# Expert routing in a fused graph network: one list of rows per expert, with the tile tables made in four portions

## The reference

```
x = x + L0_gnn(layernorm(x))     # relational graph convolution, 8 relations
x = x + L0_ffn(layernorm(x))     # feed-forward on the better-scored half of the nodes
x = x + L1_gnn(layernorm(x))     # graph attention, 4 heads
x = x + L1_ffn(layernorm(x))     # 8 experts, each node goes to its best 2

def _L1_ffn_ref(x, Wg, bg, W1, b1, W2, b2):
    gate_scores = x @ Wg + bg
    _, idx = jax.lax.top_k(gate_scores, 2)
    mask = jax.nn.one_hot(idx, 8).sum(axis=-2)
    h = jax.nn.gelu(einsum('td,edh->teh', xf, W1) + b1, approximate=False)   # 256 -> 512
    y = einsum('teh,ehd->ted', h, W2) + b2                                   # 512 -> 256
    return einsum('ted,te->td', y, mask)
```

## Time and profile before

| what | value |
|---|---|
| median of three executions | 6457.74 us |
| the profiled execution's own time | 6457.05 us |
| its span, first to last instruction | 6455.3 us |
| last stage (experts) in the span | from about 5370 us on |
| slots 0 to 19, 20 to 52, tiles after the slots | up to about 5513, to about 5850, to the end |

### The profile page before, as it was taken

How to read it: one execution, slowest core, us unless ns; L and a number is a source line. 1 busy time by engine, 2 the same in 40 slices (tenths; PEclk the granted TensorE clock), 3 DMA queues, 4 the chain that set the end, 5 groups by cost and what they waited for, 6 DMA issues and landing times. The chain is left out here.

```text
span 6455.3 us, 114956 instructions
## 1 busy us (share of the span) xinstructions
PE 4682.2 (73%) x25385; PEld 4006.7 (62%) x25386; DVE 3914.5 (61%) x11536; ACT 1836.6 (28%) x4850; POOL 4211.0 (65%) x4619
## 2 busy tenths in 40 slices
PE   9965555555555557599647777777777766899999
PEld 4435555555555556489635665665666656888998
DVE  5565555555555556733377777777777777663332
ACT  3310000000000003333234444444444444673333
POOL 1247777777777776334577777777777764785444
PEclk9987777777777778799867777767677775999999
DMA  8853333333333335411254444444444435664444
GB/s 310 318 199 104 105 105 105 104 105 105 104 104 105 105 104 166 134 42 49 85 145 117 117 117 117 117 117 117 117 117 117 117 102 171 155 156 91 72 71 67
DMA packets 366348, 786.59 MB, mean 122 GB/s; under 512 B 88338, under 2 KB 224482, under 8 KB 352612
## 3 DMA queue, kind: packets, MB, share of 16 engines
q0 software_dynamic: 209088, 520.50, 30.9%
q1 hardware_dynamic: 129524, 147.11, 7.7%
q10 hardware_dynamic: 27440, 116.02, 4.8%
HBM read 565.20 MB, written 222.43 MB: 122 GB/s over the span
## 5 line engine op out<-in xcount | busy, mean ns | idle before, releaser
L373 POOL DMA_INDIRECT s_rows<-rel_table,s_staged x1664 | 1579.8, 949 | 525.2 <-issue 485.6
L1289 POOL DMA_INDIRECT s_rows<-xp_table,s_index x1664 | 1591.4, 956 | 507.0 <-issue 444.6
L399 PE MATMUL s_part<-s_pick,s_rows 128*128 128x128 f32 x6656 | 1196.7, 353 | 909.3 <-DMA s_rows<-rel_table,s_staged 713.3
L399 PEld LDWEIGHTS s_part<-s_pick,s_rows 128*128 128x128 f32 x6656 | 1108.6, 260 | 997.9 <-DVE s_pick L407 948.8
L1412 PE MATMUL s_part<-s_pick,s_scaled 128*128 128x128 f32 x6656 | 1416.0, 369 | 373.9 <-DVE s_scaled L1577 352.9
L1412 PEld LDWEIGHTS s_part<-s_pick,s_scaled 128*128 128x128 f32 x6656 | 1182.0, 260 | 573.9 <-issue 273.2
L420 DVE TENSOR_TENSOR sums<-sums,s_part 128x256 f32 x1666 | 702.6, 422 | 930.6 <-PE s_part L399 751.5
L1592 DVE SCALAR_TENSOR_TENSOR sums<-sums,s_old_share,s_part 128x256 f32 x1666 | 794.4, 477 | 357.9 <-PE s_part L1412 221.0
L1325 ACT ACTIVATE s_apart<-window,s_local 128x128 f32<-128x128 f32 x1664 | 531.6, 390 | 1151.1 <-PE s_part L1412 1093.5
L1577 DVE TENSOR_TENSOR s_scaled<-s_rows,s_psW 128x256 f32<-128x256 f32 x1664 | 679.6, 408 | 80.7 <-issue 79.8
L407 DVE TENSOR_SCALAR s_pick<-window,s_local,s_weight 128x128 f32<-128x128 f32 x1669 | 625.5, 375 | 13.9 <-issue 0.2
(11 more groups left out here) (346 smaller groups left out, 5392.1 us busy)
## 6 DMA issues: line engine op xcount, KB each, us to landing
rel_table<-s_rows ACTq DMA_DIRECT2D x98, 1024.0 KB, 4.2
sums<-exp_rows SPq DMA_DIRECT2D x224, 132.0 KB, 2.1
s_rows<-rel_table,s_staged POOLq DMA_INDIRECT x1664, 2.7
s_rows<-xp_table,s_index POOLq DMA_INDIRECT x1664
s_edges<-edge_rows SPq DMA_DIRECT2D x208, 80.0 KB
xp_table<-s_xp ACTq DMA_DIRECT2D x49, 264.0 KB, 2.6
x_rows<-s_skip SPq DMA_DIRECT2D x49, 259.0 KB, 3.4
s_x<-in_x SPq DMA_DIRECT2D x98, 128.0 KB
```

Of the source, the lines that this page charges most:

```text
L373: pool.indirect_dma_start(out=rows[:, s, :], out_offset=None, in_=rel_table[:, :], in_offset=bass.IndirectOffsetOnAxis(ap=staged[:, 2 * s ...
L399: mm = pe.matmul(part[s % PARTS][:, k, :], rows[:, s, k * P:(k + 1) * P], pick[:, s % PICKS, :], start=True, stop=True)
L1289: pool.indirect_dma_start(out=rows[:, b * BATCH + s, :], out_offset=None, in_=xp_table[0:NR, :], in_offset=bass.IndirectOffsetOnAxis(ap=in ...
```

## The change

There is now one list per expert over all pairs, and the blank rows come once, at the very end. The table of tiles is written in four portions, when 7, 16, 25 and all 49 pairs are counted. A portion before the last holds only tiles that are already whole in the lists; how many tiles of each expert earlier portions took is kept in `taken`. The tile counts are fixed: up to 21, 57, 93 and 212 tiles. Tiles run in slots from `OPEN = 11` on, 84 of them inside the slots, 128 after.

Since two neighbouring tiles of the first 93 can hold the same node with no blank tile between, each of the first 94 adds waits until the add before it has landed. GpSimd's order in a slot becomes: add, root, two scatters, add, two scatters; the scatters are those of pair q - 3 and `moved` has five buffers. The expert weights are loaded one expert per slot in slots 0 to 7. Three of the four result buffers move to the other half of `sums`. The tables' tile numbers come from an existing constant (`window`). The last portion's eight blank writes stay where they were in SP's last slot. In the first stage, one set of blank rows is written in place of two.

```diff
-A_PAIRS = 15
-GROUP_END = [A_PAIRS, PAIRS]
-GROUP_TILES = [4 * A_PAIRS + 2 * X - 2, 4 * (PAIRS - A_PAIRS) + 2 * X - 2]
-TILES = sum(GROUP_TILES)
-LATE = 4
-SLOTS9 = PAIRS + LATE
-OPEN = A_PAIRS + LATE + 1
+CAP = NR + 2 * P
+GROUP_END = [7, 16, 25, PAIRS]
+PORTIONS = len(GROUP_END)
+TILES = 2 * NT + 2 * X
+TILES_TO = [4 * n - X + 1 for n in GROUP_END[:-1]] + [TILES]
+TILES_FROM = [0] + TILES_TO[:-1]
+SLOTS9 = PAIRS + 4
+OPEN = GROUP_END[0] + 4
-MOVED = 6
+MOVED = 5
...
# SP, slot q
-                        if q == OPEN - 2:
-                            group_in(0)
-                            for k in range(RING - 1):
-                                load_tile(k, 0, k)
-                        if q % 2 == 0 and 1 <= q // 2 <= X:
-                            load_expert(q // 2 - 1)
+                        if q < X:
+                            load_expert(q)
...
-                        if q == A_PAIRS + 2:
-                            blanks(0)
+                        if q == GROUP_END[0] + 2:
+                            group_in(0)
+                            for k in range(RING):
+                                load_tile(k, k)
+                        for g in range(1, PORTIONS - 1):
+                            if q == GROUP_END[g] + 3:
+                                group_in(g)
                         if q == SLOTS9 - 1:
-                            blanks(1)
+                            blanks()
...
# POOL
                         pool.wait_ge(ids_kept, t + 1)
-                        wait_past(pool, y_out[b], 16 * i)
+                        if isinstance(t, int) and t <= TILES_FROM[-1]:
+                            wait_past(pool, y_out[1 - b], 16 * ((t + 1) // 2))
+                        else:
+                            pool.wait_ge(y_out[b], 16 * i)
...
-                        if t is not None and t > 0:
-                            add_tile(t - 1)
-                        if 0 <= q - LATE < PAIRS:
-                            scatter(q - LATE)
                         if t is not None:
                             add_tile(t)
                         if q + 1 < PAIRS:
                             root(q + 1)
+                        if 0 <= q - 3 < PAIRS:
+                            scatter(q - 3, 0)
+                        if t is not None:
+                            add_tile(t + 1)
+                        if 0 <= q - 3 < PAIRS:
+                            scatter(q - 3, 1)
...
# VectorE, the tables of portion g
                     def tiles_of_group(g):
+                        shift = P.bit_length() - 1
+                        v.wait_ge(group_counted, g + 1)
+                        then(v.tensor_scalar(many_i[:, :], count[:, g, :], 0.0 if g + 1 < PORTIONS else float(P - 1), None, ALU.add))
+                        then(v.tensor_scalar(many_i[:, :], many_i[:, :], shift, None, ALU.logical_shift_right))
                         then(v.tensor_copy(many[:, :], many_i[:, :]))
+                        then(v.tensor_tensor(leap[:, :], many[:, :], taken[:, g, 1:X + 1], ALU.subtract))
+                        then(v.tensor_tensor(many[:, :], many[:, :], taken[:, g, 0:X], ALU.subtract))
+                        if g + 1 == PORTIONS:
+                            then(v.tensor_scalar(many[:, :], many[:, :], 1.0, None, ALU.add))
+                            then(v.tensor_scalar(leap[:, :], leap[:, :], 1.0, None, ALU.add))
                         then(v.tensor_tensor_scan(end[:, :], ones[0:1, 0:X], many[:, :], 0.0, ALU.mult, ALU.add))
+                        if g + 1 < PORTIONS:
+                            n = TILES_TO[g] - TILES_FROM[g]
+                            then(v.tensor_tensor(room[:, :], many[:, :], end[:, :], ALU.subtract))
+                            then(v.tensor_scalar(room[:, :], room[:, :], float(n), 0.0, ALU.add, ALU.max))
+                            then(v.tensor_tensor(room[:, :], room[:, :], many[:, :], ALU.min))
+                            then(v.tensor_tensor(taken[:, g + 1, 0:X], taken[:, g, 0:X], room[:, :], ALU.add))
...
-                        if q == GROUP_END[0] + 2:
-                            tiles_of_group(0)
-                            experts_of_tiles(0)
-                        if q == GROUP_END[0] + 3:
-                            rows_of_tiles(0)
+                        for g in range(PORTIONS):
+                            if q == GROUP_END[g] + 2:
+                                tiles_of_group(g)
+                                if g == 0:
+                                    v.wait_ge(unturned, OPEN + 1)
+                                experts_of_tiles(g)
+                                if g in (0, PORTIONS - 1):
+                                    rows_of_tiles(g)
+                            if q == GROUP_END[g] + 3 and 0 < g < PORTIONS - 1:
+                                rows_of_tiles(g)
```

More of the change, by code:

```diff
@@ L100, in gnn_kernel @@
     xp_table = dram("xp_table", [NR + P, EXT])
-    exp_rows = [dram(f"exp_rows{g}", [X * GROUP_CAP[g] + X * P, EXT]) for g in range(2)]
-    blank_rows = [dram(f"blank_rows{g}", [3 * P, EXT]) for g in range(2)]
+    exp_rows = dram("exp_rows", [X * CAP + X * P, EXT])
+    blank_rows = dram("blank_rows", [3 * P, EXT])
     edge_rows = dram("edge_rows", [CHUNKS, 5, P])
@@ L220, in _ @@
                     sp.wait_ge(blank_made, 1)
[L221 to L227, removed]
+                    left = exp_rows[X * CAP:X * CAP + X * P, :].rearrange("(j k p) d -> p j k d", k=2, p=P)
+                    for m in range(3):
+                        sp.dma_start(blank_rows[m * P:(m + 1) * P, :], blank[:, m % 2, :]).then_inc(blanks_out, 16)
+                    for k in range(2):
+                        sp.dma_start(left[:, :, k, :], blank[:, k, :].unsqueeze(1).broadcast_to([P, X // 2, EXT])).then_inc(blanks_out, 16)
+                    sp.wait_ge(blanks_out, 16 * 5)
                 @block.gpsimd
@@ L283, in step @@
                             pair_nodes()
-                    v.memset(blank[:, :, :, :], 0.0).then_inc(cleared, 1)
+                    v.memset(blank[:, :, :], 0.0).then_inc(cleared, 1)
                     norm(0, 0, 0)
@@ L288, in _ @@
                     v.wait_ge(blank_ids, 1)
[L289 removed]
+                    v.tensor_copy(blank[:, :, D].bitcast(I32), blank_i[:, :]).then_inc(blank_made, 1)
                     by_tiles(v, step)
@@ L1807, in gnn_kernel @@
             counts = at(st, "s9_counts", [P, 2, 2, X])
-            count = at(st, "s9_count", [P, 2, X])
+            count = at(st, "s9_count", [1, PORTIONS, X])
             place = at(st, "s9_place", [P, 2, 2, X])
@@ L2333, in rows_of_tiles @@
                     def rows_of_tiles(g):
-                        n = GROUP_TILES[g]
-                        of, to = slice(0, n), slice(g * GROUP_TILES[0], g * GROUP_TILES[0] + n)
-                        then(v.tensor_reduce(begin[:, of], over[g], AX.X, ALU.add))
-                        then(v.tensor_tensor(begin[:, of], tile_i[:, of], begin[:, of], ALU.subtract))
-                        then(v.tensor_scalar(begin[:, of], begin[:, of], float(P), None, ALU.mult))
-                        then(v.scalar_tensor_tensor(out=tile_row[:, to], in0=exp_f[:, of], scalar=float(GROUP_CAP[g]), in1=begin[:, of],
+                        n = TILES_TO[g] - TILES_FROM[g]
@@ L2340, in rows_of_tiles @@
+                        to = slice(TILES_FROM[g], TILES_TO[g])
+                        then(v.tensor_reduce(begin[g], over[g], AX.X, ALU.add))
+                        then(v.tensor_tensor(begin[g], window[0:1, 0:n], begin[g], ALU.subtract))
+                        then(v.tensor_scalar(begin[g], begin[g], taken[:, g, 0:1], float(P), ALU.add, ALU.mult))
+                        then(v.scalar_tensor_tensor(out=tile_row[:, to], in0=exp_f[g], scalar=float(CAP), in1=begin[g],
                                                     op0=ALU.mult, op1=ALU.add))
-                        v.tensor_scalar(tile_exp[:, to], exp_f[:, of], float(X - 1), None, ALU.min).then_inc(tiles_made, 1)
+                        v.tensor_scalar(tile_exp[:, to], exp_f[g], float(X - 1), None, ALU.min).then_inc(tiles_made, 1)
```

148 lines of the change are left out of this document (66 added, 82 removed).

## The result

The changed kernel took 6383.17 us (median of three, 6373.09 to 6386.11) against 6457.74 before: a ratio of 0.9881, 95% interval 0.9867 to 0.9895. It cost 22 us where 29 were forecast, and a gain that the forecast had at nothing paid for about half of it.

A forecast was written before the change was run, and what follows sets the result against it. The prediction took the middle tile slots to be bound by GpSimd at 10.1 us. Its terms, -44.8 - 34.5 + 29 - 5.7 + 5 + 2 + 4 - 3 = -48.0, gave 6410 us, range 6376 to 6444.

The forecast's parts named there:

- Fewer tiles and nine more tile slots: Last stage: 12 fewer tiles at the end, -44.8 us; tiles from slot 11 instead of 20, -34.5 us.
- The adds one at a time: GpSimd in tile slots: waiting for each add's landing costs 0.7 us per slot over 42 slots, +29 us (0 to 80).
- The same instructions, so its own sum stays: GpSimd's new order in a tile slot: its summed time per slot was claimed unchanged, 10.14 us.
- Hidden wait: Rival, tile slots: adds land early enough that none waits, slots stay at 10.1 us; 6381 us, chance 0.2.
- Five buffers: Scatters one slot earlier with MOVED 6 to 5: still covered, also in slots without tiles; 0 (to +3) us.
- Weights: Slots 0 to 7, one expert's weights per slot: DMA at 97% of full, barely fits; +4 us (0 to +15).
- Its last line: Signs of being wrong: tile slots stay at 10.1 us or pass 12, or slots 1 to 8 leave 6.5.
- As before two slots lie between: Moved buffers: from a pair's scatters to its buffer's rewriting, over 10 us against landings of 2.7 to 6.3.
- The opening: From slot 9's mark to the first tile slot: 16.8 us against 22.5 before; -5.7 us (-12 to +3).
- First stage: End of the first stage: five of ten blank DMAs go, shortening the wait for a table store; -3 us (-6 to 0).
- Tables of portions 1 and 2: Slots 18 and 27: VectorE's table work and SP's wait for the finished table; 2 * 2.5 = +5 us (0 to +12).
- The close: Last slot: blank writes stay in SP's queue, VectorE's table block grows from 5.5 to about 7.5; +2 us (0 to +6).

## Why the prediction was right, point by point

- **Fewer tiles and nine more tile slots** (-44.8 and -34.5): the rate at the end held, 3.73 us per tile. The run with tiles from slot 20 bears the nine slots out roughly: 46 us apart, less the 16 to 18 behind the slots, are 28 to 30, where its forecast had 31.
- **The adds one at a time** (+29): mechanism right, size a third too high. The run with two in flight puts it at +22. From a landing to the start of the next add the trace has 0.79 us (0.83 forecast), and landings in the tile slots have a mean of 4.3 us (4.2 in the row of before, half a microsecond more assumed). Two of them with 0.79 each make 10.2 us, more than TensorE's 9.67: by this sum the chain of adds comes near to being a bound of its own, which the forecast saw only as a wait inside GpSimd's sum. As forecast, the wait is the longer before even adds (0.66 us of idle time, 0.58 before odd ones).
- **"The same instructions, so its own sum stays"**: this step failed. GpSimd's busy time in a tile slot was 8.42 us; it is 7.98 with the new order alone and 8.15 in the changed kernel, as scatters meet VectorE's copies less often or at cheaper places. In the kernel before, without the wait, the order brings the slot to 9.67 to 9.73, TensorE's bound. This is the term that was missing: in the changed kernel 0.27 us per slot, some 11 us in 42. For the slots' wait and the tables together 29 + 5 us were forecast, and 0.36 in 38 slots came, 13.7. Of these 20 us, by which the forecast was too high, the missing term is 11 and the wait's size 7. The changed kernel without its wait is at 9.95 and not at 9.7; that difference was not followed beyond the slots with the tables.
- **Hidden wait** (first rival): its time is met within 2 us, its mechanism isn't. That the total came so near to it is chance: the tile slots took 10.47 us, between its 10.1 and the forecast's 10.8.
- **Five buffers, "0 (to +3)"**: wrong, +5 by the marks of the same eight slots (56.1 for 51.0). **Weights, +4**: 7.0 us per slot came as forecast, for the wrong reason. Six buffers give it back, a stretch with more traffic has none of it, and the DMA share in these slots is 0.77, where the prediction looked for one above 0.9. Its last line also counts slots 1 to 8 leaving 6.5 as a sign of being wrong, though its own +4 makes them 7.0; they did leave it, and what was wrong is this step. "As before two slots lie between" overlooked that the scatters had gone from the head of a slot to its end.
- **The opening**, -5.7: measured 26.6 us from slot 9's mark to slot 11's, 39.8 before from slot 17's to slot 20's, less a slot of 6.48: -6.7.
- **First stage**, -3: -5.1 (387.4 against 392.6).
- **Tables of portions 1 and 2**: TensorE stood 2.19 us at 5534.8 for VectorE's block, and the slots with the two tables took 12.5 and 12.0 us of a mean of 10.47, about 3.5 us together where 5 were forecast; that SyncE's table wait adds to it isn't borne out by moving it. **The close**, +2: +2.2, by the result of the last slot tile (33.0 us behind slot 49's mark, 30.8 before).

In sum: -5.6 us at the mark of slot 1, +4.2 in slots 1 to 8 (against 6.48 per slot throughout), -6.7 in the opening, +13.7 in 38 tile slots, +2.2 at the close, and with the -44.8 and -34.5 that makes -71.5 of the span's -73.9 (6455.3 to 6381.4). The other 2.4 us lie behind the slots (526.5 us from slot 49's mark to the end, 638.5 before, where 30 tiles of 3.73 less and the close make -109.7 of -112.0) and were not followed further. What stays open is why single tile slots swing between 8.3 and 12.5 us: the landings swing too, from 3.7 to 6.3, but that the one makes the other was not shown.

## What to carry to other kernels

Where a queue is the bound, its instructions have no fixed length: look at what else runs beside each one, and at which point of it, because a new order can shift them out of, or into, another engine's way. To test whether one instruction holds up another, compare their ends: if one keeps a fixed distance behind the other, it waited for it. A wait for a landing in every step makes a chain of its own, landing plus restart, and that chain is to be compared with every other bound before it is charged to one engine. When a release moves from the head of a step to its end, a buffer that was two steps away is only one away.

## What was not expected of the hardware

A scatter's descriptors took 0.99 us alone and 1.30 on average beside a VectorE copy of 1028 columns in the kernel before, up to 1.52; an add took 1.61 alone and up to 2.13. The same copy cost nothing when it started in a scatter's first 0.2 us or an add's first 0.4. DMA traffic of 296 GB/s at a share of 0.89 lengthened none of slots 1 to 8 in the run with the old order (6.41 us each, 6.38 before). And one chip ran the whole program at 7732 us for 6457, with a mean granted clock of 0.73 for 0.81, while its last stage kept its pace (996.2 us from slot 1's mark, 994.5 for the same kernel elsewhere).
